# Attention of 16 heads: scores in two row tiles of float32r, the sums of two key tiles back to back

## The reference

```python
def reference(x, W_qkv, b_qkv, ...):
    xn = _layernorm(x)
    return x + attn(xn, W_qkv, b_qkv) + ffn(xn, ...)

def attn(x, W_qkv, b_qkv):              # B, D, N = 2, 4096, 256; H = 16, p = 16
    qkv = (x @ W_qkv + b_qkv).reshape(B, D, 3, H, p).transpose(2, 0, 3, 1, 4)
    q, k, v = (qkv[0], qkv[1], qkv[2])
    scores = jax.nn.softmax(jnp.einsum('bhip,bhjp->bhij', q, k), axis=-1)
    out = jnp.einsum('bhij,bhjp->bhip', scores, v)

def ffn(x, ...):                        # 256 -> 1024 -> 256
    h = x @ W_exp + b_exp
    h = butterfly(h, up_weights)
    h = gelu(h + up_bias)
    h = butterfly(h, down_weights)
    return h @ W_con + b_con + down_bias
```

## Time and profile before

| | |
|---|---|
| median of 3 runs | 6592.78 us (6592.01 to 6596.98) |
| span of the profiled execution | 6591.0 us |
| PE, DVE, ACT busy | 98%, 80%, 72% of the span |
| mean granted TensorE clock | 0.984 of 2.4 GHz |
| share of the attention's regions (line 590, 4096 of them) | 4820.9 us of DVE |

### The profile page before, as it was taken

One profiled execution on the slowest core, in us unless ns is written; L12 is line 12 of the kernel. 1 busy time (PEld: TensorE's weight loads), 2 busy tenths in 40 slices (PEclk: granted clock), 3 DMA queues, 4 the chain that ended last, 5 costly groups with the idle time before them and its releaser, 6 DMA issues. The chain is left out here.

```text
span 6591.0 us, 114833 instructions
## 1 busy us (share of the span) xinstructions
PE 6469.5 (98%) x35808; PEld 2072.2 (31%) x35808; DVE 5269.1 (80%) x5256; ACT 4748.4 (72%) x8645; POOL 479.8 (7%) x355
## 2 busy tenths in 40 slices
PE   9799999999999999999999999999999999999999
PEld 5222222222222222222222222222222222222498
DVE  8888888888888888888888888888888888888333
ACT  5277777777777777777777777777777777777744
POOL 4599000000000000000000000000000000000000
PEclk9699999999999999999999999999999999999999
DMA  8412000000000000000000000000000000000011
GB/s 246 132 45 67 13 12 10 12 13 12 11 5 12 13 12 10 12 13 12 11 5 12 13 12 10 12 13 12 11 5 12 13 12 10 12 12 3 17 45 41
DMA packets 234283, 158.46 MB, mean 24 GB/s; under 512 B 171584, under 2 KB 212928, under 8 KB 228032
## 3 DMA queue, kind: packets, MB, share of 16 engines
q1 hardware_dynamic: 230208, 127.56, 7.8%
q0 software_dynamic: 3456, 23.07, 1.0%
HBM read 99.76 MB, written 50.33 MB: 23 GB/s over the span
## 5 line engine op out<-in xcount | busy, mean ns | idle before, releaser
L590 DVE TENSOR_REDUCE maxima<-psum 128x1 f32<-128x1024 f32 x4096 | 4820.9, 1219 | 964.2 <-PE psum L682 963.4
L576 ACT ACTIVATE arena<-psum 128x512 f32<-128x512 f32 x8192 | 4443.6, 594 | 1492.4 <-PE psum L704 1481.3
L704 PE MATMUL psum<-arena 98*128 98x512 bf16 x8192 | 3126.1, 384 | 49.2 <-ACT arena L576 44.6
L682 PE MATMUL psum<-arena 96*128 96x512 bf16 x8192 | 2819.3, 385 | 24.5 <-DVE maxima L590 17.4
L714 PE MATMUL psum<-arena 128*32 128x512 f32 x16384 | 2194.7, 608 | 0.6 <-ACT arena L576 0.6
L704 PEld LDWEIGHTS psum<-arena 98*128 98x128 bf16 x8192 | 794.1, 97 | 2850.4 <-ACT arena L576 2318.6
L682 PEld LDWEIGHTS psum<-arena 96*128 96x128 bf16 x8192 | 800.9, 99 | 596.0 <-DVE maxima L590 97.9
L714 PEld LDWEIGHTS psum<-arena 128*32 128x32 f32 x16384 | 322.9, 108 | 874.3 <-ACT arena L576 856.9
L924 ACT ACTIVATE gelus<-psum,bias_up 128x512 f32<-128x512 f32 x128 | 88.3, 690 | 189.2 <-PE psum L888 187.4
L966 DVE TENSOR_TENSOR hidden_low<-gelus,hidden_high 128x512 fp32r<-128x512 f32 x128 | 88.6, 692 | 100.7 <-ACT hidden_high L927 100.7
L900 PE MATMUL psum<-w_down_low,hidden_high 128*128 128x256 f32 x512 | 144.9, 283 | 0.0
(11 more groups left out here) (85 smaller groups left out, 1409.7 us busy)
## 6 DMA issues: line engine op xcount, KB each, us to landing
q_parts<-arena SPq DMA_DIRECT2D x32, 384.0 KB, 5.5
k_parts<-arena SPq DMA_DIRECT2D x32, 384.0 KB, 3.9
arena<-k_parts SPq DMA_DIRECT2D x32, 384.0 KB
arena<-q_parts SPq DMA_DIRECT2D x64, 192.0 KB
planes<-in_up_planes POOLq DMA_DIRECT2D x10, 1024.0 KB, 5.1
planes<-in_down_planes POOLq DMA_DIRECT2D x10, 1024.0 KB, 5.0
y<-in_x SPq DMA_DIRECT2D x16, 512.0 KB, 5.0
xn_transposed<-arena SPq DMA_DIRECT2D x16, 512.0 KB, 5.3
```

The lines of the kernel that those rows point to most:

```text
L576: nc.scalar.activation(probs[:, kt % 4, BANK * g:BANK * g + BANK], score_bank(g, is_wide(c, kt, last)), ACT.Exp).then_inc(s_exp, 1)
L590: nc.vector.tensor_reduce(maxima[:, parity, n:n + 1], ps_max[n % 2].rearrange("p a b -> p (a b)"), axis=AX_X, op=ALU.max).then_inc(s_regio ...
L682: mm = nc.tensor.matmul(ps_max[n % 2][:, half, :], q_rows[c][0:ROWS, P * t:P * t + P], k_rows[c // 2][0:ROWS, keys:keys + BANK], start=Tru ...
L704: nc.tensor.matmul(score_bank(g, wide), k_rows[c // 2][0:ROWS + MAX_PARTS, P * kt:P * kt + P], q_rows[c][0:ROWS + MAX_PARTS, BANK * g:BANK ...
```

## The change

**Parts.** q and k are split into two float32r parts instead of three bfloat16 ones, and three products of parts are summed instead of six: 48 rows (`ROWS = 3 * HD`), 50 with the maximum. The parts are stored as 4-byte numbers. ACT writes the first part from PSUM, DVE the second with one operation (`low_part`).

**Row tiles.** The lower 64 partitions of `k_rows` hold keys 0 to 2047, the upper 64 keys 2048 to 4095; q stands in both. A region's two halves are now one matmul in the lower and one in the upper half of the array's rows. Scores alternate likewise: score `e` takes key tile `u` of the lower half when `e` is even, of the upper half when it is odd.

**Order.** Work goes by turns of two key tiles (one of each half): eight scores, four regions, then the eight sums of both key tiles directly behind each other. Per region PE does score, upper half, lower half, score. Scores run six ahead (`LEAD`), regions 14 (`AHEAD`). Each of the eight exponentials of a turn frees one of three banks, in rotation, also in the last superblock.

**Maxima.** The transposed maxima no longer have a bank: they are an item of their own in the ring of the two region slots, after four regions of the next superblock (`TURN_POS`), 65 items to a superblock. `place_neg` issues two DMAs, and the rows of ones are brought by four.

```diff
-    PARTS = 3
-    ROWS = 6 * HD
+    PARTS = 2
+    ROWS = 3 * HD
...
-    AHEAD = 10
-    BEHIND = 6
+    HALF_N = N // 2
+    HALF_P = P // 2
+    UNITS = KT // 2
+    EXPS = QG * KT
+    ITEMS = REGIONS + 1
+    TURN_POS = 4
+    AHEAD = 14
+    BEHIND = 4
+    LEAD = 6
...
         def load_q(sp, head, half, slot):
-            for first, part, copies in ((0, 0, 3), (3, 1, 2), (5, 2, 1)):
...
+            for lower in (0, HALF_P):
+                for first, part, copies in ((0, 0, 2), (2, 1, 1)):
...
-                        nc.scalar.activation(dst, src, ACT.Identity, bias=bqk[:, m:m + 1]).then_inc(s_full, 1)
...
-                        nc.scalar.copy(parts[:, PARTS * m, :], full[:, m, :]).then_inc(s_high, 1)
+                        nc.scalar.activation(in_chunk_order(m, parts[:, PARTS * m, :]), from_chunk(m),
+                                             ACT.Identity, bias=bqk[:, m:m + 1]).then_inc(s_high, 1)
...
+                def low_part(c, m):
+                    dve.wait_ge(s_high, 2 * KD * c + m + 1)
+                    high = in_chunk_order(m, parts[:, PARTS * m, :].bitcast(F32))
+                    nc.vector.scalar_tensor_tensor(in_chunk_order(m, parts[:, PARTS * m + 1, :]), from_chunk(m),
+                                                   bqk[:, m:m + 1], high, ALU.add, ALU.subtract).then_inc(s_parts, 1)
...
                 def step(s, c, i, last):
-                    for kt in range(KT):
-
-                        act.wait_ge(s_pv, KT * s + kt + 1)
+                    for u in range(UNITS):
                         for g in range(QG):
...
+                            for half in range(2):
+                                e = 2 * QG * u + 2 * g + half
+                                if g == 0:
+                                    act.wait_ge(s_pv, KT * s + 2 * u + half + 1)
+                                act.wait_ge(s_score, EXPS * s + e + 1)
+                                nc.scalar.activation(probs[:, (2 * u + half) % 4, BANK * g:BANK * g + BANK],
+                                                     ps_s[:, score_bank(c, e), :], ACT.Exp).then_inc(s_exp, 1)
...
+                def region_half(c, pos, slot, half):
+                    t, keys = region_at(pos) // 4, region_at(pos) % 4 * BANK
+                    lower = HALF_P * half
+                    return nc.tensor.matmul(ps_max[slot][:, half, :], q_rows[c][lower:lower + ROWS, P * t:P * t + P],
+                                            k_rows[c // 2][lower:lower + ROWS, keys:keys + BANK], start=True, stop=True)
...
+                def score(s, c, e, first=False):
...
+                    if not first or e > 2:
+                        pe.wait_ge(s_exp, EXPS * s + e - taken_back(c, e) + 1 + 4)
...
+                    done = 0
+                    for k in range(REGIONS):
+                        d, pos = divmod(AHEAD + done, ITEMS)
+                        to = c + 1 + d
+                        if pos == TURN_POS and not (last and to >= 4):
+                            neg_to_rows(s + d, item(s + 1 + d, pos), slot_of(to, pos))
...
+                        if more:
+                            score(s1, c1, e1)
+                        if region:
...
+                            pe.wait_ge(s_region_free, number + 1)
+                            region_half(to % 4, pos, slot, 1)
+                            region_half(to % 4, pos, slot, 0).then_inc(s_region, 1)
+                        if more:
+                            score(s1, c1, e1 + 1)
+                        if k % 4 == 3:
+                            sums(s, c, k // 4, 0)
+                            sums(s, c, k // 4, 1)
```

More of the change, by code:

```diff
@@ L96, in attention_and_butterfly_ffn @@
         planes = sb("planes", [P, 2, 4, PAIRS], until=before_ffn)
[L97 to L118, removed]
+        fold = sb("fold", [P, 3, PAIRS], until=before_ffn)
@@ L149, in attention_and_butterfly_ffn @@
[L149 to L153, removed]
+        wqkv = sb("wqkv", [P, KD, 3 * D], until=prepare)
+        bqk = sb("bqk", [P, 2 * KD], until=prepare)
+        bv = sb("bv", [P, D], until=prepare)
+        btail = sb("btail", [P, 2, D], until=prepare)
+        stats = sb("stats", [P, 2 * CT, 6], until=prepare)
+        mv = sb("mv", [P, 2 * CT, 2], until=prepare)
@@ L169, in attention_and_butterfly_ffn @@
+        def load_k(sp, head, slot):
+            rows = bass.ds(HD * head, HD)
+            for half in range(2):
+                for first, count in ((0, 2), (2, 1)):
+                    src = k_dram[0:count, rows, HALF_N * half:HALF_N * half + HALF_N]
+                    lower = HALF_P * half + HD * first
+                    sp.dma_start(k_rows[slot][lower:lower + HD * count, :].bitcast(F32), src).then_inc(s_k[slot], 16)
         ps_xt, ps_qk, ps_v = psum[:, 0:2, :], psum[:, 2:6, :], psum[:, 6:8, :]
@@ new lines, in _ @@
+                for n in range(REGIONS):
+                    reduce_region(n, n, n % 2, 0)
+                for pos in range(AHEAD + BEHIND):
+                    handle(1, 1, pos, first=True)
+                def step(s, c, i, last):
+                    for r in range(ITEMS):
+                        d, pos = divmod(AHEAD + BEHIND + r, ITEMS)
+                        to = c + 1 + d
+                        if not last or to < 4:
+                            handle(s + 1 + d, to % 2, pos)
+                        elif to == 4 and r == ITEMS - BEHIND - 2:
+                            m = SUPER - 1
+                            negate(m, item(SUPER, 0) - 1, 1)
+                            high_part(m)
+                            low_part(m)
+                            copy_rows(m, item(SUPER, 0), slot_of(0, 0))
+                        if r == ITEMS - BEHIND - 1:
+                            turn(s)
+                        if r == ITEMS - BEHIND:
+                            invert(s)
+                        if r == ITEMS - BEHIND + 1:
+                            scale(s)
+                        if r == ITEMS - BEHIND + 2:
+                            add(s)
@@ L749, in step @@
                                 pe.wait_ge(s_q[to % 4], 16 * LOADS * (i + 1 + to // 4))
                                 pe.wait_ge(s_k[to // 2 % 2], 16 * LOADS * (i + 1 + to // 4))
-                            halves += [(4 * i + to, to % 4, n, h) for h in range(2)]
-                        more = not (last and c == 3)
-                        rows = s + 1 if kt == ROWS_KT and more else None
-                        if rows is not None:
-                            neg_to_rows(rows, QG * (KT * s + kt) + 2)
@@ L767, in step @@
-                        if kt1 or more:
-                            scores(s1, c1, kt1, 0, wide and is_wide(c, kt, last))
-                            for h in halves[3:4]:
-                                region_half(*h)
-                            scores(s1, c1, kt1, 1, wide, rows)
-                            if wide:
-                                if not is_wide(c, kt, last):
-                                    pe.wait_ge(s_region_free, REGIONS * SUPER + 2)
-                                scores(s1, c1, kt1, 2, wide)
-                                scores(s1, c1, kt1, 3, wide)
```

363 lines of the change are left out of this document (162 added, 201 removed).

## The result

The changed kernel takes 7886.16 us (median of 4 runs, 7884.43 to 7894.71) against 6594.63 us for the kernel before (4 runs): a ratio of 1.196, 95% interval 1.194 to 1.198. That lies outside the predicted range. The profiled execution has a span of 7883.3 us.

What follows compares the result with a forecast made beforehand. PE was taken to bound the kernel before; after the change, a ring through two region slots and the sums, 5.72 us a turn. 6591 + 20 + 26 + 5 = 6642 us profiled, 6644 us median; range 6410 to 7120 us.

Steps and rivals of the forecast that it cites:

- The clock: Rival, 8%: TensorE streams 62% of the time instead of 92%, clock falls to 1.2 GHz; up to +3300, about 9900 us.
- The sum of a superblock: Attention: 16 turns 91.5 us plus 1.4 for transposed maxima, 92.9 against 92.59; times 63, about +20 us.
- What bounds the kernel before: Attention before the change: PE sets the pace without a hole, 2.84 us a key tile, 5.68 us per two.
- The pairs overlap: Scores and regions: lower and upper row-tile matmuls run at once, a turn's 16 becoming 8 pairs, 1.82 us.
- the price of no overlap: Rival, 12%: row tiles don't run at once; 6.17 us a turn, +454, about 7100 us.
- The ring of two slots with the sums inside: Turn of two key tiles: sums keep PE from refilling region slots; 5.72 us, DVE idle about 1.0 us.
- The 0.105 us for weights that can't be loaded ahead: Charged in a turn wherever PE comes out of a wait or a changeover: 0.105 us each.
- Weights are loaded ahead: Rival, 17%: idle row tile takes weights while PE waits; turn 5.51 us, -212, about 6430 us.
- dearer edges: Rival, 14%: pairs at 0.3 us or costlier row/column tile changeovers; 5.85 to 6.1 us a turn, 6780 to 7030 us.
- ACT's ring: Exponentials' pace, shorter than DVE's ring; holds in the last superblock without regions: 5.42 us a turn, +26 us.
- Preparation: Before attention: larger stores, +12 us at worst, -10 at best, taken as +5 us.
- The turning point: Attention gets slower by this mechanism alone once a pair loses over some 0.03 us against full overlap.

Runs made afterwards that it cites:

- e2_fill: Changed kernel with each half of a turn's second and third region multiplied three times, 8 matmuls more a turn: 6758.33 us, 1.025 of the kernel before.
- e5_full_rows: As e3_one_tile, but every score and region matmul takes 112 or 114 rows at once: 7190.85 us, 1.091 of the kernel before.
- e4_half_reduce: Changed kernel with DVE reducing only the first bank of a slot, 512 of 1024 columns: 6631.17 us (one run).
- e3_one_tile: Changed kernel with every score and region matmul in the lower row tile, so no two can overlap: 9661.46 us, 1.466 of the kernel before.
- e7_short_sums: Changed kernel with exponentials and v in bfloat16, so the sums take one pass: 6792.42 us, 1.030 of the kernel before.

## Why the prediction was wrong, point by point

- **The clock**: this is the step that failed, and nine tenths of the miss. It stood among the rivals with 8%, outside the range, with its mechanism half right (a lower load lets the clock fall, but load was taken as time with a matmul streaming). Its price was bracketed loosely ("up to +3300 us") for a clock low throughout; what came was a clock that falls and rises every second turn or so, with most turns between 5.7 and 7.8 us. The step of the maxima came out as 112.35 us instead of 92.9: (112.35 - 92.9) x 63 = 1225 us, which with the forecast 6642 makes 7867 of the measured 7883. e2_fill, with the clock nearly always up, has a step of 94.7, so some 1.8 x 63 = 111 us of the 1225 aren't the clock; the other 1114 are.
- **The sum of a superblock**: it left out a term that it had itself read. Of the 92.59 us before, the prediction gives 90.9 to key tiles and "1.7 us the rest", and the new sum of 91.5 + 1.4 has no such rest: the term was put at nothing without a reason. The rest is the stop at every fourth superblock (6.8 us there, 1.7 for each), and it stayed. In e2_fill a superblock is (6266.8 - 303.2) / 63 = 94.7 us; 16 turns of 5.70 are 91.2, the item of transposed maxima costs 1.3 in its turn and 0.1 in the last (1.4 forecast, right), and some 2.1 is left. 2.1 x 63 = 132 us more than covers the 114 us by which e2_fill lies above 6644.
- **What bounds the kernel before**: not contradicted; nothing tested it by itself.
- **The pairs overlap**: right. The upper half and the score start at 4518.18 both. e5_full_rows gives the price of no overlap as forecast, 6.17 us a turn, and 7191 us against "about 7100" (the rest that was left out is in it too).
- **The ring of two slots with the sums inside**: right to 0.03 us: 5.72 forecast, 5.69 in the changed kernel at full clock, 5.70 in e2_fill. The 0.105 us for weights that can't be loaded ahead is in it and fits: the pair after the first starts 4518.52 - 4518.18 = 0.34 us behind it, 0.11 more than 0.227. Without both such terms the turn would be 5.51. "Weights are loaded ahead" and "dearer edges" didn't happen.
- **ACT's ring**: right, 5.42 forecast and 5.43 in e4_half_reduce. It holds in the last superblock too where the clock is up: in e5_full_rows the sums there start 5.44 us apart (6746.96 and 6752.40). In the changed kernel the clock is down there as well, and its turns take 6.8 to 7.8 us.
- **Preparation**: +5 forecast, and the attention begins 2.8 us later (first region 225.7 against 222.9 us).
- **Why the chance was too small**: I measured activity as time with a matmul streaming (62% against 92%). e3_one_tile, with more time streaming than the changed kernel and a clock of 0.69, shows that this is the wrong measure, and e5_full_rows shows what was left out of it: matmuls of 96 rows became matmuls of 48, which is what row tiles are for. Streaming the same matmuls in pairs or one by one changes the share of time and not the work in a turn. The rows already said that the new load would lie in untested ground, between one that stayed at 0.50 and one that rose. A case for which no row stands on either side deserved a bigger share than 8%, and the range its price.
- **The turning point** ("once the pair loses more than some 0.03 us") doesn't follow from the sum beside it: with no loss at all the turn was already 5.72 against 5.68. Measured, the change is worth nothing at full clock (2.5% slower in e2_fill), since the time that row tiles take off PE comes back as the block of sums in the ring. With the sums apart it is worth 4%.

What stays open: at which load exactly the clock turns, whether overlap counts beside the rows and the length of the turn, what makes the engines stop where the loop goes around, and whether the tiling mode has a part in e3_one_tile beside the rows.

## What to carry to other kernels

A change that makes TensorE's work smaller (row tiles, fewer passes, fewer rows) can take its clock away, and then its matmuls take about twice as long (the 16 records of the sums 3.62 us instead of 1.92); before counting a gain, look for a stretch of the same kernel with a load as low as the new one, and give the clock a rival's full price if there is none. Where a clock row reads between its two levels, compare turns at full clock with the forecast before doubting the mechanism: here the ring was right within 1%. What the old kernel's period has beyond its repeated pattern belongs in the new kernel's sum too, unless the change removes it. When an engine works in order and a ring of few buffers runs through it, a long block belongs in pieces between the refills, and if the clock still falls, useless matmuls can pay for themselves.

## What was not expected of the hardware

- The rows in use count, not only the time. 16 matmuls of 48 to 50 rows in a turn, in pairs: clock 0.823. One behind the other, all in one tile, in a longer turn: 0.692. One behind the other over 112 to 114 rows, the turn as long: 0.985.
- More work, less time: 8 added matmuls a turn took the clock from 0.823 to 0.973 and 1128 us off; 12 added, with fill in the last superblock, took it from 0.542 to 0.953 and 775 us off.
- PE's share of busy time was 97 to 98% in the kernel before and in the changed one, and in e7_short_sums, at half clock throughout, a window of 4000 us shows 3927 us busy. It doesn't see any of this.
